# A conditioned feed-forward kernel: W3 loaded and projected whole ahead of the first product, loads and first tiles reordered, three joined orders changed

## What is computed

```python
# x: 16 x 512 x 1024, cond: 16 x 512, all float32
q = relu(cond @ W3 + b3)                         # 16 x 1024
v = (n * x + sum_over_tokens(x)) * q[:, None]    # n = 512 tokens
y = relu(v @ W2 + b2)                            # 1024 x 1024 weights
base = y @ W_base + b_base
shared = (y @ A_s) @ B_s                         # rank 16
gates = softmax(y @ W_router + b_router)         # 6 experts, the best 2 are kept
routed = sum over experts of gate * (y @ A_r) @ B_r
out = x + base + shared + routed
```

## Time and profile before

| | |
|---|---|
| median of 3 runs | 1420.25 us (1420.07 to 1420.95) |
| the profiled execution | 1420.39 us, its span 1418.5 us |
| granted TensorE clock | 1.000 over the span |
| loads and stores | 200.03 MB, mean 141 GB/s |

### The profile page before, as it was taken

One profiled execution on the slowest core, in us unless ns is written; L12 is line 12 of the kernel. 1 busy time (PEld: TensorE's weight loads), 2 busy tenths in 40 slices (PEclk: granted clock), 3 DMA queues, 4 the chain that ended last, 5 costly groups with the idle time before them and its releaser, 6 DMA issues.

```text
span 1418.5 us, 18155 instructions
## 1 busy us (share of the span) xinstructions
PE 1408.9 (99%) x6186; PEld 1156.4 (82%) x6186; DVE 897.3 (63%) x1529; ACT 682.5 (48%) x1312; POOL 27.1 (2%) x57
## 2 busy tenths in 40 slices
PE   8999999999999999999999999999999999999998
PEld 5878888888888888888887888888888888888887
DVE  6976566665656656566879665564656546556563
ACT  6894856748567484775544132332313223132230
POOL 3100000000000000000000000000000000000000
PEclk9999999999999999999999999999999999999999
DMA  8242514424143241426726527164262733617242
GB/s 312 90 141 75 159 50 118 141 81 155 49 140 109 87 156 47 146 98 219 259 93 193 212 62 272 64 213 146 97 245 67 236 113 130 219 60 261 88 151 87
DMA packets 135580, 200.03 MB, mean 141 GB/s; under 512 B 38880, under 2 KB 38880, under 8 KB 135488
## 3 DMA queue, kind: packets, MB, share of 16 engines
q1 hardware_dynamic: 135488, 198.87, 42.2%
HBM read 127.12 MB, written 71.70 MB: 140 GB/s over the span
## 4 chain that ended last, share of the span: by engine, by line
PE 94%; DVE 2%; ACT 1%; issue 1%; SPq 1%; DMA 1%; ACTq 0%; DVEq 0%
PE ps L1560 31%; PE ps L1562 31%; PE ps L1561 31%; ACT src L635 0%; DMA w_raw<-in_w 0%; ACT src L627 0%; PE ps L1568 0%; DVE act_lo L1059 0%; ACT act_hi L667 0%; ACT yhi L686 0%; DVE src L1070 0%; DVE w_lo L1298 0%; DVE buf L1104 0%; SPq L313 0%; DVE wl_raw L1311 0%
## 5 line engine op out<-in xcount | busy, mean ns | idle before, releaser
L1560 PE MATMUL ps<-act_hi,w_hi 128*128 128x512 f32 x1792 | 697.6, 389 | 0.3 <-DVE w_lo L1298 0.3
L1561 PE MATMUL ps<-act_lo,w_hi 128*128 128x512 f32 x1792 | 697.2, 389 | 0.0
L1562 PE MATMUL ps<-act_hi,w_lo 128*128 128x512 f32 x1792 | 697.2, 389 | 0.0
L1560 PEld LDWEIGHTS ps<-act_hi,w_hi 128*128 128x128 f32 x1792 | 336.3, 188 | 71.6 <-DVE act_lo L1059 1.1
L1562 PEld LDWEIGHTS ps<-act_hi,w_lo 128*128 128x128 f32 x1792 | 336.3, 188 | 70.0
L1561 PEld LDWEIGHTS ps<-act_lo,w_hi 128*128 128x128 f32 x1792 | 336.3, 188 | 69.8
L667 ACT ACTIVATE act_hi<-src 128x512 fp32r<-128x512 f32 x380 | 232.3, 623 | 256.0 <-PE ps L1562 254.2
L1059 DVE TENSOR_TENSOR act_lo<-src,act_hi 128x512 fp32r<-128x512 f32 x320 | 217.5, 685 | 108.1 <-ACT act_hi L667 107.2
L1104 DVE SCALAR_TENSOR_TENSOR buf<-ps,bb_sb,buf 128x512 f32<-128x512 f32 x128 | 96.0, 750 | 161.5 <-PE ps L1562 145.7
L1059 DVE TENSOR_TENSOR act_lo<-buf,act_hi 128x512 fp32r<-128x512 f32 x64 | 43.4, 687 | 86.8 <-ACT act_hi L667 86.7
L686 ACT ACTIVATE yhi<-buf 128x512 fp32r<-128x512 f32 x128 | 80.0, 625 | 35.6 <-PE ps L1562 34.8
(11 more groups left out here) (107 smaller groups left out, 962.1 us busy)
## 6 DMA issues: line engine op xcount, KB each, us to landing
src<-in_xT SPq DMA_DIRECT2D x224, 256.0 KB, 3.0
y_scratch<-buf SPq DMA_DIRECT2D x128, 256.0 KB, 2.3
src<-y_scratch SPq DMA_DIRECT2D x128, 256.0 KB, 5.2
outT<-buf SPq DMA_DIRECT2D x128, 256.0 KB, 3.9
buf<-in_xT SPq DMA_DIRECT2D x32, 256.0 KB, 5.1
wl_raw<-in_wbase SPq DMA_DIRECT2D x6, 1024.0 KB, 5.8
r<-in_w SPq DMA_DIRECT2D x16, 256.0 KB, 8.5
grow<-gates_scratch SPq DMA_DIRECT2D x96, 32.0 KB, 2.1
```

What stands on the lines that cost most here:

```text
L1560: nc.tensor.matmul(out, wh, a_h, start=start, stop=False, skip_group_check=onto)
L1561: nc.tensor.matmul(out, wh, a_l, start=False, stop=False, skip_group_check=onto)
L1562: return nc.tensor.matmul(out, wl, a_h, start=False, stop=stop, skip_group_check=onto)
```

## The change

W3's second half is loaded ahead of x, and projected before the first half's `condition` is through; the tiles of G11 are taken one at a time (sum, mean, scaling, high, low) instead of all sums first; x's G12 and G22 are loaded ahead of Q21 and Q22; the sums of G12 move from ScalarE to DVE, and their shift on GpSimd ahead of the casts of s2; s1 and s2 are made tile by tile. In the joined orders, t1 of the second pair stands behind the others' work, the last pair has `y_low` ahead of `c21`, and hb_hi of the first pair of stage 2 comes after the fourth high part instead of before it. Six warm-up matmuls go.

```diff
@@ SP
             load_w3(0)
+            load_w3(1)
             for k in range(H):
                 load_x(0, G11, k)
                 load_w2(Q11, r11, k)
-            load_w3(1)
             for k in range(H):
                 load_x(0, G21, k)
                 load_w2(Q12, r12, k)
             for k in range(H):
-                load_w2(Q21, r21, k)
-                load_w2(Q22, r22, k)
-            for k in range(H):
                 load_x(0, G12, k)
             for k in range(H):
                 load_x(0, G22, k)
+            for k in range(H):
+                load_w2(Q21, r21, k)
+                load_w2(Q22, r22, k)
@@ GpSimd
             pool.wait_ge(q_ready, 2)
             shift_of(0, G21)
+            shift_of(0, G12)
             for k in range(H):
                 pool.wait_ge(s2_made, k + 1)
                 w2_high(2, s2, k)
                 if k == 1:
-                    shift_of(0, G12)
-            shift_of(0, G22)
+                    shift_of(0, G22)
@@ ScalarE
-            first_w2(0)
-            first_w2(1)
-            for k in (2, 3):
-                t = tile(G11, k)
+            def first_total(k):
+                t = tile(G11, k)
                 act.wait_ge(x_loaded[t], 16)
                 nc.scalar.activation(src[:, t, :], src[:, t, :], ACT.Copy,
-                                     accum_out=vsum[:, t:t + 1]).then_inc(first_sum, 1)
-            for k in range(2, H):
-                first_w2(k)
-            for k in range(H - 1):
-                first_hi(k)
+                                     accum_out=vsum[:, t:t + 1]).then_inc(later_sums, 1)
+
+            first_w2(0)
+            first_total(1)
+            first_hi(0)
             act.wait_ge(q_sum, 2)
             nc.scalar.activation(qrow[:, D // 2:D], ps[0:NB, Q_BANK + 1, :], ACT.Copy).then_inc(q_copied, 1)
-            first_hi(H - 1)
+            first_w2(1)
+            first_total(2)
+            first_hi(1)
+            first_w2(2)
+            first_total(3)
+            first_hi(2)
+            first_w2(3)
+            x_sum(0, G21, 0)
+            first_hi(3)
+            for k in range(1, H):
+                x_sum(0, G21, k)
             for k in range(H):
-                x_sum(0, G21, k)
-            x_scale(0, G21)
-            for k in range(H):
+                x_scale(0, G21, (k,))
                 high(0, 1, k, True)
-            for k in range(H):
-                x_sum(0, G12, k)
...
-                    if j == 2:
+                    if j == 2 and p > 0:
                         lr_high_b(p)
+                if p == 0:
+                    lr_high_b(0)
                 copy_u4(g, H - 1)
@@ DVE
-            dve.wait_ge(bias_loaded, 16)
-            for k in (0, 1):
-                t = tile(G11, k)
-                dve.wait_ge(x_loaded[t], 16)
-                nc.vector.reduce_sum(vsum[:, t:t + 1], src[:, t, :], axis=AX.X).then_inc(first_sum, 1)
             dve.wait_ge(q_sum, 1)
             nc.vector.tensor_copy(qrow[:, 0:D // 2], ps[0:NB, Q_BANK, :]).then_inc(q_copied, 1)
-            first_w2_low(0)
+            dve.wait_ge(x_loaded[tile(G11, 0)], 16)
+            nc.vector.reduce_sum(vsum[:, H * G11:H * G11 + 1], src[:, tile(G11, 0), :], axis=AX.X).then_inc(first_sum, 1)
+            dve.wait_ge(bias_loaded, 16)
             condition(0)
...
             for k in range(H):
                 t = tile(G11, k)
+                if k == 0:
+                    dve.wait_ge(first_sum, 1)
+                else:
+                    dve.wait_ge(later_sums, k)
+                nc.vector.tensor_scalar(shift[:, t:t + 1], vsum[:, t:t + 1], 1.0 / T, None,
+                                        ALU.mult).then_inc(first_mean, 1)
+                dve.wait_ge(first_mean, k + 1)
+                dve.wait_ge(q_ready, 1)
                 nc.vector.tensor_scalar(src[:, t, :], src[:, t, :], shift[:, t:t + 1], qn[:, k, 0:1],
                                         ALU.add, ALU.mult).then_inc(first_x1, 1)
-                if k >= 1:
-                    low(0, 0, k - 1)
-                if k >= 2:
-                    first_w2_low(k)
-            low(0, 0, 3)
-            w2_low(1, r12, (0,))
-            condition(1)
-            w2_low(1, r12, (1, 2, 3))
+                first_w2_low(k)
+                low(0, 0, k)
+                if k == 2:
+                    condition(1)
+
+            def b_sum(k):
+                t = tile(G12, k)
+                dve.wait_ge(x_loaded[t], 16)
+                nc.vector.reduce_sum(vsum[:, t:t + 1], src[:, t, :], axis=AX.X).then_inc(b_summed, 1)
+
+            w2_low(1, r12, (0, 1))
+            b_sum(0)
+            b_sum(1)
+            w2_low(1, r12, (2, 3))
+            low(0, 1, 0)
+            b_sum(2)
+            low(0, 1, 1)
+            b_sum(3)
+            low(0, 1, 2)
+            low(0, 1, 3)
             for k in range(H):
                 dve.wait_ge(w2_loaded[H * Q21 + k], 16)
                 dve.wait_ge(w2_loaded[H * Q22 + k], 16)
                 nc.vector.tensor_tensor(s12[:, k, :], r21[:, k, :], r22[:, k, :], ALU.add).then_inc(s1_made, 1)
-            for k in range(H):
-                low(0, 1, k)
-            for k in range(H):
                 dve.wait_ge(s1_made, k + 1)
                 nc.vector.tensor_tensor(s2[:, k, :], s12[:, k, :], r11[:, k, :], ALU.subtract).then_inc(s2_made, 1)
...
                     c21(0, 1)
-                    t1(1, 1)
                     low(1, 0, 2)
-                    t1(1, 2)
                     y_low(0, C22, 3)
+                    low(1, 0, 3)
                     c21(0, 2)
-                    low(1, 0, 3)
-                    t1(1, 3)
+                    for j in range(1, H):
+                        t1(1, j)
                 else:
                     for j in range(H):
                         low(i + 1, 0, j)
-                        if j > 0:
+                        if j > 0 and i == LAST:
+                            y_low(i, C22, j)
+                            c21(i, j - 1)
+                        elif j > 0:
                             c21(i, j - 1)
                             y_low(i, C22, j)
@@ PE
             project(0, range(QK))
-            warm(6)
+            project(1, (0, 1))
             pe.wait_ge(const_step, 3)
             turn(0)
+            project(1, range(2, QK))
             warm(4)
-            project(1, range(QK))
```

More of the change, by code:

```diff
@@ L190, in adaln_ffn @@
         first_sum = sem("first_sum")
+        later_sums = sem("later_sums")
+        b_summed = sem("b_summed")
         first_mean = sem("first_mean")
@@ L281, in tile_no, with sum_no @@
             return H * source_no(i, q) + k + 1
+        def sum_no(i, q, k):
+            if i == 0:
+                return H * (G21, G22).index(q) + k + 1
+            return tile_no(i, q, k) - H
         def x1_no(i, q, k):
@@ L588, in shift_of @@
             def shift_of(i, q):
-                pool.wait_ge(x_summed, tile_no(i, q, H - 1))
+                if i == 0 and q == G12:
+                    pool.wait_ge(b_summed, H)
+                else:
+                    pool.wait_ge(x_summed, sum_no(i, q, H - 1))
                 ks = slice(H * HALF_OF[q], H * HALF_OF[q] + H)
@@ L633, in x_scale @@
                     t = tile(q, k)
-                    act.wait_ge(x_summed, tile_no(i, q, k))
+                    if i > 0 or q != G12:
+                        act.wait_ge(x_summed, sum_no(i, q, k))
                     nc.scalar.activation(src[:, t, :], src[:, t, :], ACT.Identity, bias=shift[:, t:t + 1],
@@ L1206, in _ @@
+            nc.vector.reduce_sum(vsum[:, H * G11:H * G11 + 1], src[:, tile(G11, 0), :], axis=AX.X).then_inc(first_sum, 1)
+            dve.wait_ge(bias_loaded, 16)
             condition(0)
-            first_w2_low(1)
-            dve.wait_ge(first_sum, H)
-            nc.vector.tensor_scalar(shift[:, H * G11:H * G11 + H], vsum[:, H * G11:H * G11 + H], 1.0 / T, None,
-                                    ALU.mult).then_inc(first_mean, 1)
-            dve.wait_ge(first_mean, 1)
-            dve.wait_ge(q_ready, 1)
```

## The result

The changed kernel takes 1422.37 us (median of 22 runs, 1421.26 to 1423.91) beside 1420.22 us for the kernel before on the same chip (22 runs, 1419.75 to 1421.73): ratio 1.0013, 95% interval 1.0007 to 1.0019. That is 2.15 us more, inside the 0.2% which the prediction called no change, and inside its range. It is still a real loss, since the interval leaves out 1, and it is 1.8 us more than was forecast. The profiled execution took 1422.18 us with a span of 1420.3.

The account below looks back on a forecast made before the run. TensorE bounds the kernel, busy 1408.9 of 1418.5 us, with DVE setting product 2. Product 2's 2.2 us delay less 1.85 from the joined orders gives +0.35 on 1420.39: 1420.6 us, range 1418.0 to 1423.2.

Parts of the forecast that it names:

- Start of product 0: First matmul of product 0 at 14.95 us instead of 17.85, 2.9 us earlier.
- Product 2: Start of product 2, set by DVE: t1 at 39.3, product 2 at 42.6, 2.2 us later than before.
- the ledger: Count of DVE's work from 12.85 us to t1: 23.3 us without casts, 3.2 more with them.
- Casts: GpSimd's eight weight casts slow DVE ahead of t1: 0.46 us each, seven counted, 3.2 us.
- The joined orders: Three reorderings on DVE and ScalarE that shorten PE's waits after product 2: together 1.85 us gained.
- (a): PE's wait at 103.60 us for C22's last buf_lo goes, a new one comes at C21's first: gain 0.3 us.
- (c): PE's two waits at 765.79 and 767.03 us, hanging on ScalarE's high part of tile 3, go: gain 1.1 us.
- (b): Last pair: buf_lo goes before the bank's 0.66 us, so PE's idle 0.19 us ends: gain 0.45 us.
- GpSimd starved: Slower rival: DVE shuts out GpSimd's shift of G21 near 23.4 us, product 2 2.5 us later, 1423.1; chance 0.08.
- The clock: Slower rival: PE's wait before product 2 drops the clock, fourteen matmuls cost 2.8 us more, 1423.4; chance 0.11.
- what would show it: Signs of right: product 0 at 15, product 2 at 42.6, PE idle 0.8 before product 1, expected later waits.
- "wrong": Signs against: product 2 before 40, clock under 1.00 after 38 us, or DVE idle over 1.5 us before product 1.

Follow-up runs that it names:

- the fill: Changed kernel with 16 matmuls on zeros, which add nothing, put in PE's wait between products 1 and 2: 1420.10 us, ratio 0.9996.
- the one with t1 moved: Kernel before with the three joined orders, t1 of the second pair's tiles 2 and 3 moved behind C21's first low part: 1417.46 us.
- the start rebuilt from the runs: New start with Q21, Q22 loaded before G12, G22, s1 in DVE's waits, G12's sums on ScalarE; joined orders, t1 moved: 1419.64 us.

## Why the prediction was right, and where it was off

**Start of product 0: right.** 14.65 for a forecast 14.95. From DVE's first sum to PE it took 3.38 us for a forecast 3.35; the rest is the load, whose landing moves by more than that from execution to execution. PE's listed waits for W3 fell from 1.9 to 0.7 us.

**Product 2: the sum right, by luck in its terms.** t1 at 38.84 for 39.3, product 2 at 42.23 for 42.6, +1.8 for +2.2. But the ledger counted DVE's instructions from 12.85 on as one stream without waits but for 0.4 and 0.5 us, with **the four sums of G12 as 2.4 us of it**. The runs show that this term is worth nothing here: without the sums product 2 stands where it stood (27.58 after product 0 both times), because ScalarE's 1.37 us per tile sets the low parts of product 1, and the sums fill the holes. The ledger came out right since DVE's stream with the sums ends at the same time as that chain, which is a coincidence. So is the rest: from 12.34 to 38.84 the trace has 26.5 us, as forecast, but its short waits for high parts come to 1.2 us instead of 0.4, and the casts to some 2.4 instead of 3.2. What sets t1 is: ScalarE's chain to the last low part (ends 29.8), then s1, s2 and w_low, 7.7 us, then 1.3 us that GpSimd's casts add. ScalarE's chain begins where DVE's scaling of G11's last tile ends, so the first half of the ledger still matters. The sentence "ScalarE loses the four sums of G12, and is ahead of DVE" was the mistake: ScalarE is the later one in product 1.

**Casts: the term was 3.2 us in all (0.46 each, seven of eight).** For the four casts of s2 the price is measured, 1.3 us, 0.32 each. Those of product 1's weights were not tried alone; the DVE rows beside them are longer than their like by 1.1 us together (0.92 at 18.07 and 1.10 at 20.17 instead of 0.68, the pair at 21.80 1.70 instead of 1.28).

**The joined orders: right.** (a) 0.26 for 0.3, with the new wait of 0.64 at buf_lo where 0.7 to 0.8 was forecast; (c) 1.16 for 1.1, both waits gone. (b) gave 0.29 for 0.45 in this one profile: DVE's buf_lo(C22, 0) at 704.20 waited for a store to land, so the pieces behind it were 0.3 late and the slow first step of 0.34 stayed. In the nine other profiles with this order (b) gave 0.42 to 0.46.

**GpSimd starved: did not happen.** The shift of G21 took 0.64 us. The prediction let this hang on the sums of G12, which read one operand. The run with the sums on ScalarE takes that cause away: there the shift took 0.63 us amid w_low instructions with two operands. So it was not the sums that let it through; the 2.2 and 2.7 us in the earlier trace rows need a cause that no run here shows.

**The clock: the step that failed.** The rival was described much as it came (about 4 us of wait, which were 4.5, and 0.2 us more per matmul, which started every 0.43 us instead of 0.23), but it had a chance of 0.11 and a price of 2.8 us. By their mean clock of 0.997 to 0.999 it happened in all 22 runs. Its price in the trace was 1.58 us, nine matmuls instead of fourteen; in medians 2.3, as the fill shows. The likely reason for the difference is that the profiled run is a mild one: it has a mean clock of 0.999, as seven others do, while fourteen of the 22 have 0.997 or 0.998 and a median 0.6 us higher, and a profile with 0.997 (below) has its clock at one half for twice as long. "Against: the wait of 1.3 us leaves the clock alone, and a longer one no row shows" took the silence of the trace for evidence. In its place the six profiles with an unfilled wait of 3.1 us or more before product 2 all show half clock in it or behind it; two of the eleven runs with the casts on ScalarE, whose wait is 3.23 us, kept a mean clock of 1.000. The Trainium skill (TensorE: Matmul & The Clock Gate, HAM oscillation) was the better guide: it describes waits for loads that put the array back to half rate, and the trace agrees, with waits of 3.1 to 4.9 us in six kernels, though here PE waits for a low part of DVE. That the time still fell into the range is luck as well: the range was set to leave this rival out, at 1423.4, and held it only because its price was smaller and product 2 came 0.4 us earlier. The trace ends at +1.87 where +0.35 was forecast; these 1.5 us are 1.6 of the clock and 0.2 lost at (b), less 0.4 that product 2 was earlier, and 0.2 by which the lag grew slowly between (a) and (b).

**Of "what would show it"** these came true: product 0 near 15, product 2 at 42.2, DVE hardly idle from 20 to 42, the wait near 110, none near 767. PE's loss before product 1 was 0.26 (0.49 from start to start, less 0.23), not 0.8. One sign of "wrong" came too: a clock under 1.00 after 38 us.

## What to carry to other kernels

An early start is worth only as much as the engine that feeds the next stage can follow: here 3.2 us gained at product 0 became 5 us of waiting, and the wait took the clock as well. When a change opens a wait of some microseconds on PE, give the clock its own term, and if the wait can't be closed, fill it with matmuls that change nothing. Before an instruction is priced by its duration, look at whether its engine waits for another one there: the same four sums cost nothing with ScalarE taking tiles one by one, and by the rows 1.2 us with its scalings first.

## What the hardware showed that was not expected

- The clock need not fall in the wait. In the changed kernel the granted clock is 1.00 through all of the wait of 4.51 us and falls at 42.5, 0.2 us after PE's first matmul; in the kernel with the casts on ScalarE it fell 1 us after PE had taken up product 2. With the scalings first it fell in the wait, at 41.4 (windows as above):

```profile
38.00:42.00 4.00, 1.36 (x7) 0.78 (x5) 3.96 (x6) 0.52 (x2) 0.39 (x1) 0.93 0.01 2
42.00:46.00 4.00, 2.55 (x6) 2.07 (x7) 3.90 (x8) 3.99 (x7) 0.00 (x0) 0.50 0.01 2
46.00:50.00 4.00, 4.00 (x14) 3.11 (x14) 3.90 (x7) 2.78 (x5) 1.83 (x3) 0.72 0.00 0
```

- How long it stayed low came in two sizes. In these three rows 0.07, 0.50 and 0.28 of 4 us are missing from 1.00; twice that is the time at one half, 6.8 us. It was as long in the kernel with the sums on ScalarE. In the other four kernels with a fall it was 3.4 us (0.43 of the 4 us from 42 to 46 in the changed kernel). The waits were 4.1 and 4.9 us with the long stretch, and 4.5, 4.5, 3.2 and 3.1 with the short one, so the length of the wait does not tell which comes. Part of the long stretch passes while PE stands still: the price is 2.3 and 2.5 us there, and 1.6 with the short one.
- The mean granted clock helps even in its third digit, with care. In the second group of runs it separates the two groups of times of the kernel before and of the one with t1 moved (1.000 and 0.999, some 2 us apart). But three runs of the kernel before in the other groups have 0.999 and are fast (1419.85, 1419.96, 1420.28), and a fall behind PE's last matmul, where it costs PE nothing, counts too: in the start rebuilt from the runs that matmul starts at 1413.61, and the clock is at one half again from 1416.4 on. Nor does the figure show everything: it is 1.00 in the first warm-ups, whose matmuls start every 0.42 us.
- A GpSimd cast of s2 beside DVE instructions with two operands lasted 1.01 us and lengthened the DVE instruction beside it from 0.69 to 0.98; with the casts on ScalarE that row is 0.69 again. The Trainium skill (SBUF — State Buffer, Who interferes with whom) says that such instructions contend with GpSimd's reads, and the trace agrees: 0.3 us per cast for DVE.
